# A blockwise scan with ten columns a state instead of eleven

## What is computed

```python
def step(h, inp):
    dA_t, dB_t, x_t, C_t, t = inp
    h = h * dA_t + dB_t * x_t[:, :, None]
    nrm = jnp.sqrt(jnp.sum(h * h, axis=(1, 2), keepdims=True))
    fac = jnp.minimum(20.0 / (nrm + 1e-08), 1.0)
    h = jnp.where(t % 10 == 0, h * fac, h)
    y = jnp.einsum('bdn,bn->bd', h, C_t) + D_param * x_t
    return (h, y)
```

## Time and profile before

| | |
|---|---|
| median of 3 runs | 1531.29 us (1530.69 to 1533.32) |
| the profiled execution, its own time | 1536.68 us |
| its span in the profile | 1534.8 us |
| mean granted TensorE clock | 0.991 |
| PE, DVE, ACT, POOL busy, share of the span | 95%, 82%, 73%, 61% |

### The profile page before, as it was taken

How to read it: one execution, slowest core, us unless ns; L and a number is a source line. 1 busy time by engine, 2 the same in 40 slices (tenths; PEclk the granted TensorE clock), 3 DMA queues, 4 the chain that set the end, 5 groups by cost and what they waited for, 6 DMA issues and landing times.

```text
span 1534.8 us, 25461 instructions
## 1 busy us (share of the span) xinstructions
PE 1455.1 (95%) x6902; PEld 1020.6 (66%) x6902; DVE 1255.2 (82%) x2526; ACT 1121.2 (73%) x2618; POOL 939.6 (61%) x956
## 2 busy tenths in 40 slices
PE   6999999999979999999999999999999998999998
PEld 5555555555467777777777777777666666677776
DVE  6685566745479999999999999999999998788884
ACT  4444455455999999999999999999999964334243
POOL 0224313432269999999999999999999997400000
PEclk9999999999999999999999999999999999999999
DMA  8215437453757667666666666666545447466420
GB/s 269 83 49 176 131 103 198 139 178 115 233 137 208 169 165 188 168 172 167 172 165 181 177 162 181 157 173 172 133 111 112 95 105 224 116 221 193 150 84 28
DMA packets 231557, 236.28 MB, mean 154 GB/s; under 512 B 46040, under 2 KB 197272, under 8 KB 231416
## 3 DMA queue, kind: packets, MB, share of 16 engines
q1 hardware_dynamic: 230472, 233.34, 54.4%
q10 hardware_dynamic: 944, 1.31, 0.2%
HBM read 136.31 MB, written 98.56 MB: 153 GB/s over the span
## 4 chain that ended last, share of the span: by engine, by line
DVE 35%; POOL 14%; PE 12%; issue 5%; DVEq 1%; POOLq 1%; DMA 1%; ACT 0%; SPq 0%; ACTq 0%
DVE h L1346 22%; POOL rc L1110 13%; DVE banks L1336 8%; PE banks L1495 4%; PE banks L1516 3%; PE banks L1526 3%; DVE qs L1330 2%; PE banks L1170 1%; DVEq L1344 1%; DMA ub<-scratch_ub 1%; DVE q_ln_st L1772 1%; DVE q_g L1681 1%; POOLq L1118 1%; DVE q_x L1653 1%; PE banks L1536 0%
## 5 line engine op out<-in xcount | busy, mean ns | idle before, releaser
L1346 DVE TENSOR_TENSOR_SCAN h<-decay,banks 128x352 f32<-128x352 f32 x820 | 710.4, 882 | 57.4 <-DVE banks L1336 2.9
L1121 POOL TENSOR_TENSOR hc<-h,bc 128x640 f32<-128x640 f32 x410 | 593.3, 1447 | 0.0
L1170 PE MATMUL banks<-hc,w_ident 128*128 128x320 f32 (+1 forms) x1664 | 526.6, 440 | 0.1
L1239 ACT ACTIVATE tb<-dtc,a 128x320 f32<-128x320 f32 (+1 forms) x832 | 417.2, 555 | 4.8 <-DVE x L612 4.8
L1170 PEld LDWEIGHTS banks<-hc,w_ident 128*128 128x128 f32 x1664 | 285.0, 191 | 70.7 <-issue 0.8
L1261 ACT ACTIVATE decay<-tb 128x640 f32<-128x640 f32 x410 | 294.9, 723 | 0.0
L1110 POOL TENSOR_TENSOR rc<-qs,w_mhalf 128x1 f32<-128x1 f32 x410 | 225.8, 551 | 110.5 <-DVE qs L1330 110.5
L1156 PE MATMUL banks<-ub 128*128 128x176 f32 x1640 | 273.5, 289 | 2.4 <-DMA ub<-scratch_ub 2.4
L1149 PEld LDWEIGHTS banks<-sc_ss,sc_ones 128*128 128x128 f32 x820 | 123.5, 189 | 158.2 <-ACT sc_sq L1250 152.2
L1156 PEld LDWEIGHTS banks<-ub 128*128 128x128 f32 x1640 | 217.6, 193 | 2.6 <-DMA ub<-scratch_ub 2.6
L1149 PE MATMUL banks<-sc_ss,sc_ones 128*128 128x1 f32 x820 | 151.8, 254 | 37.7 <-ACT sc_sq L1250 19.5
(11 more groups left out here) (133 smaller groups left out, 1818.5 us busy)
## 6 DMA issues: line engine op xcount, KB each, us to landing
ub<-scratch_ub SPq DMA_DIRECT2D x410, 107.5 KB
bc<-scratch_blk SPq DMA_DIRECT2D x205, 160.0 KB, 3.5
scratch_ub<-turned SPq DMA_DIRECT2D x64, 512.0 KB, 3.6
scratch_ub<-spread SPq DMA_DIRECT2D x64, 176.0 KB, 2.6
scratch_xc<-xc SPq DMA_DIRECT2D x8, 1024.0 KB, 4.8
scratch_sg<-sg SPq DMA_DIRECT2D x8, 1024.0 KB, 6.0
piece<-scratch_u SPq DMA_DIRECT2D x32, 256.0 KB, 4.0
q_ys<-scratch_y SPq DMA_DIRECT2D x8, 1024.0 KB, 5.7
```

The source lines that it names most:

```text
L1121: pool.tensor_tensor(hc[:, pl % 2, :, at * S:(at + 1) * S] .rearrange("p (c b n) e -> p c b n e", c=KE, b=B)[:, :, b], state(m)[:, :, 0:S] ...
L1170: mm = pe.matmul(banks[:, y_bank(p), 0:KE * B * wide], w.ident[:], rhs, start=(n == 0), stop=(n == N - 1))
L1239: act.activation(tanh_rows(c, r), dtc[:, c % 2, k * B:(k + 1) * B, 0:blocks_of(c) * S].rearrange("p b (k e) -> p k b e", e=S), ACT.Tanh, s ...
L1346: dve.tensor_tensor_scan(state(m).rearrange("p r e -> p (r e)")[:, half], decay[:, m % DRING, half], psI[m % B][:, half], 0.0, ALU.mult, A ...
```

## The change

The scan block shrinks to the ten times 10j+1 to 10j+10, so a row has W = 10 columns. What column 0 did is now done in three places. VectorE multiplies the last column of the unit before by the decay of the first time of the block (`first_step`, into `hd`). `carry` multiplies that by the factor and adds it to column 0 of the input in PSUM. And since the state at 10j+10 leaves the scan unscaled, its output has to be scaled later: all factors are kept (`rcs`), and GpSimd multiplies each tenth output by its factor in the post stage (`scale_ends`). The output at time 0 is made once (`first_output`). ScalarE makes the first decays of 4 blocks and both batches in one exp of 512 elements (`first_d`). The halves of the scan are 24 and 40 rows instead of 32 and 32. The decay ring has 5 places instead of 6.

```diff
-W = S + 1
+W = S
-DRING = 6
+DRING = 5
+FG = 4
+LEAD = 24
-    HR = NCH // 2
+    HALVES = (slice(0, LEAD), slice(LEAD, NCH))
...
 def scalar(act, pre, post):  # decays(m)
+            if k % FG == 0 and b == 0:
+                if group_of(j) >= 2:
+                    act.wait_ge(hd_ready, (j - (FG if k else (blocks_of(c - 1) - 1) % FG + 1)) * B)
+                dst, src = first_of_group(j)
+                act.activation(dst, src, ACT.Exp, scale=DTA_HALF / SHARP).then_inc(first_ready, 1)
             act.activation(
                 decay[:, m % DRING].rearrange("p (g i e) -> p g i e", g=DB, e=W)[:, :, :, 1:],
-                tanh_block(j, b), ACT.Exp, scale=DTA_HALF / SHARP).then_inc(decay_ready, 1)
+                tanh_block(j, b)[:, :, :, 1:], ACT.Exp, scale=DTA_HALF / SHARP).then_inc(decay_ready, 1)
...
         def carry(m):
-            b = m % B
+            j, b = m // B, m % B
+            dve.wait_ge(hd_ready, m + 1)
             dve.wait_ge(norm_ready, m + 1)
             dve.wait_ge(inp_ready, m + 1)
-            dve.tensor_scalar(inp(m)[:, :, 0], state(m - B)[:, :, S], rc[:, b:b + 1], None, ALU.mult
-                              ).then_inc(carry_ready, 1)
+            dve.scalar_tensor_tensor(out=inp(m)[:, :, 0], in0=hd[:, b, :], scalar=rcs[:, j, b:b + 1],
+                                     in1=inp(m)[:, :, 0], op0=ALU.mult, op1=ALU.add).then_inc(carry_ready, 1)
+
+        def first_step(m):
+            for x in range(2):
+                dve.wait_ge(h_ready[x], m + 1)
+            dve.wait_ge(first_ready, group_of(m // B) + 1)
+            dve.tensor_tensor(hd[:, m % B, :].rearrange("p (g i) -> p g i", i=GR),
+                              state(m - B)[:, :, W - 1].rearrange("p (g i) -> p g i", i=GR),
+                              first_decays(m // B, m % B), ALU.mult).then_inc(hd_ready, 1)
...
+        first_step(0)
         for m in range(UNITS):
             carry(m)
+            if m + 1 < UNITS:
+                first_step(m + 1)
             scan(m, 0)
             if B <= m + 1 < UNITS:
                 clamp(m + 1)
...
 def gpsimd(pool, post):  # scan stage
         def norm(m):
-            b = m % B
-            if m >= B:
-                pool.wait_ge(carry_ready, m - B + 1)
+            j, b = m // B, m % B
             pool.wait_ge(q_held, m + 1)
-            pool.tensor_tensor(rc[:, b:b + 1], qs[:, b:b + 1], w.mhalf[:, 0:1], ALU.pow).then_inc(norm_ready, 1)
+            pool.tensor_tensor(rcs[:, j, b:b + 1], qs[:, b:b + 1], w.mhalf[:, 0:1], ALU.pow).then_inc(norm_ready, 1)
...
+            if m == UNITS - 17:
+                post.scale_ends(pool, 0)
...
 def gpsimd(pool):  # post stage
+        scale_ends(pool, 1)
+        rstd(0)
         for i in range(TILES):
-            rstd(i)
+            if i + 2 < TILES:
+                scale_ends(pool, i + 2)
+            if i + 1 < TILES:
+                rstd(i + 1)
+
+    def scale_ends(pool, i):
+
+        j0 = -(-i * TT // S)
+        j1 = -(-(i + 1) * TT // S)
+        at = ys[i % 2][:].rearrange("p k (b t) -> p k b t", b=B)[:, :, :, j0 * S - i * TT::S]
+        pool.wait_ge(y_in[i % 2], 16 * (i // 2 + 1))
+        pool.tensor_tensor(at, at, scan.rcs[:, j0:j1].rearrange("p j b -> p b j").unsqueeze(1)
+                           .broadcast_to([P, KE, B, j1 - j0]), ALU.mult).then_inc(scan.ends_scaled, 1)
```

More of the change, by code:

```diff
@@ L700, in vector @@
                 scan.decay_scale(dve)
+                scan.first_output(dve)
                 post.residual_steps(dve)
@@ L728 @@
 Scan = namedtuple("Scan", """sync gpsimd tensor scalar vector load_first load_units tanhs decay_rates decay_scale masks
-    decay_ready y_out y_copied squares load_piece turn_piece high_piece low_piece store_piece ut_lo
+    first_output rcs ends_scaled decay_ready y_out y_copied squares load_piece turn_piece high_piece low_piece store_piece ut_lo
     spread_b store_b copy_bt b_split""")
@@ L808, in scan_stage @@
     qs = own.put("qs", [P, B])
-    rc = own.put("rc", [P, B])
+    rcs = own.put("rcs", [P, NB, B])
+    hd = own.put("hd", [P, B, NCH])
+    c0 = own.put("c0", [P, B, N, 2])
+    s0 = own.put("s0", [P, B])
+    y0 = own.put("y0", [P, KE * B])
     u0 = own.put("u0", [P, KE * B, 2])
@@ L814, in scan_stage @@
     h = second.put("h", [P, 2, B, NCH, W])
+    first_d = second.put("first_d", [P, 2, DB * FG * B * GR])
     hc = second.put("hc", [P, 2, ROWS, QB * S])
@@ L903, in load_first @@
         for b in range(B):
-            sp.dma_start(b0[:, b], dram["bc"][0:N, b:b + 1, 0:2].rearrange("n b t -> b n t")
-                         .broadcast_to([P, N, 2])).then_inc(s_in, 16)
+            for tile, n0 in ((b0, 0), (c0, N)):
+                sp.dma_start(tile[:, b], dram["bc"][n0:n0 + N, b:b + 1, 0:2].rearrange("n b t -> b n t")
+                             .broadcast_to([P, N, 2])).then_inc(s_in, 16)
         sp.wait_ge(blk_out, 32)
@@ L1344, in scan @@
                 dve.wait_ge(carry_ready, m + 1)
-            half = slice(x * HR * W, (x + 1) * HR * W)
+            half = slice(HALVES[x].start * W, HALVES[x].stop * W)
             dve.tensor_tensor_scan(state(m).rearrange("p r e -> p (r e)")[:, half], decay[:, m % DRING, half],
@@ L1636, in skip_first @@
         if k == 0:
-            dve.wait_ge(y_in[0], 16)
+            dve.wait_ge(scan.ends_scaled, 1)
         dve.wait_ge(scaled, k + 1)
@@ L1820, in _ @@
                 pre.gpsimd(pool, scan)
-                scan.gpsimd(pool)
+                scan.gpsimd(pool, post)
                 post.gpsimd(pool)
```

71 lines of the change are left out of this document (52 added, 19 removed).

## The result

The changed kernel takes **1801.54 us** (median of 4 runs, 1800.58 to 1802.44); the kernel before takes 1530.99 beside it. The ratio is 1.1772, with a 95% interval of 1.1756 to 1.1788. Its profiled execution took 1801.09 us around a span of 1799.2, so 264.4 us more than the span of before; the forecast had +267 for it.

The account below looks back on a forecast made before the run. Bound: the scan stage's loop through VectorE and GpSimd, 2.178 us a unit. New unit 1.77 + 0.20 + 0.58 + 0.28 = 2.83 us; 408 × 0.65 = +266 us, giving 1798 us; range 1735 to 1880.

Parts of the forecast that it names:

- Weigh, 0.51 and 1.447: GpSimd in the scan loop: weigh starts 0.51 us behind the power and lasts 1.447, to 1.96, still 640 elements.
- Carry: VectorE in the scan loop: after a second half of 0.91 us, carry starts at 0.68, so first_step is up at 0.94.
- The hold, released 0.19 before weigh's end: VectorE's first_step waits for weigh, begins in effect at 1.77 us, so VectorE stands still for about 0.8 us.
- The low end of the range: Product at 0.225 us and weigh's early release partly in proportion to its length, 0.33 instead of 0.19: unit 2.68, time 1735.
- Product, 0.20 of interval: VectorE's first_step: own time 0.28 us, next instruction starting about 0.08 before its end, so 0.20 of the unit.
- First half and clamp to power, 0.58 + 0.28: End of the scan unit: first half of 240 elements takes 0.58 us, then clamp, then 0.28 to the next power.
- The first rival (no meeting): Scan loop: first_step and weigh do not meet; VectorE's loop 2.02 us, unit 2.1, time 1515 us; chance 0.08.
- the chance of 0.06 for faster: Whole kernel: the forecast's chance that the change makes it faster, beside same 0.02 and slower 0.92.
- The clock rival: TensorE in the scan stage falls to half clock as it rests more; 1935 us with half the stage so; chance 0.08.
- The second rival's partial hold: Scan loop: weigh holds the ports for a part only; unit 2.2 to 2.6 us, some 1550 to 1700 us; chance 0.09.

Follow-up runs that it names:

- e10_flat: Kernel before with weigh reading the first 640 elements of the state in one piece instead of ten of each eleven columns; 1536.98 us.
- e2_add_sbuf: Kernel before with a product added behind the carry, the state's last column times an SBUF factor, result unused; 1879.81 us.
- e7_late24: Changed kernel with first_step moved from in front of the scan's first half to behind the clamp; 1604.22 us, ratio 1.0456.
- e6_wait_back: Changed kernel with the wait on the carry of two units before put back ahead of GpSimd's power; 1829.04 us.
- e1_psum: Changed kernel with first_step's second factor read from PSUM instead of first_d in SBUF, leaving out the first decay; 1540.16 us, 1.005 times before.

## Why the prediction was right

The range, the side and the mechanism held, and the number to 4 us. That it came so close is partly luck, since two terms were off by 0.08 to 0.10 us a unit and cancel; either alone would have moved the time by 30 to 40 us. By the steps, counted from the power:

1. *Weigh, 0.51 and 1.447.* The start is right (0.516). The length is 1.542: "it is still 640 elements" left out that the rows now touch, and e10_flat shows the price of that, 0.10. This is the step that failed: **+0.095**.
2. *Carry.* The second half's interval was given as 0.91 and is 0.89, and the carry starts at 0.74 instead of 0.68, since the clamp is nearer to the power. It takes 0.257, which is what the working took (0.26). None of it is on the path: the product is up 0.40 into weigh instead of 0.43, and its end does not move with that.
3. *The hold, released 0.19 before weigh's end.* Right, and firmer than it was put. Over 407 products the end lies 0.08 behind weigh's (0.078 to 0.087); with 0.27 of its own it begins in effect 0.19 before weigh's end. That beginning is worked out; the trace shows the ends. It is 0.08 for weighs of 1.20 us, of 1.44 (e2_add_sbuf) and of 1.54, and for products that were up 0.31, 0.39 or 0.56 into them. The low end of the range assumed a release in proportion to weigh's length; the distance is the same for all three lengths.
4. *Product, 0.20 of interval.* 0.19 by the timeline (1003.26 less 1003.07). Its own time is 0.27 where nothing holds it (e7_late24), near the 0.28 of the strided row and above the 0.224 of the formula, which the Trainium skill, "VectorE: DVE Perf Modes", section on the TRN2 errata, states for an fp32 add.
5. *First half and clamp to power, 0.58 + 0.28.* The half is 0.57. Clamp to power is 0.20: the diff takes a wait out ahead of the power, which the working did not price. e6_wait_back puts it back and finds 0.065 to 0.07. The rest goes with a clamp of 0.126 us instead of 0.134: e2_add_sbuf has the wait and a clamp of 0.127, and clamp to power is 0.27 there. **-0.08**.

The sum is 0.516 + 1.542 - 0.19 + 0.19 + 0.57 + 0.20 = 2.83. Weighing the rule of the Trainium skill against the row was worth its place: by a hold for the whole instruction, as that page has it, the forecast would have been 1876 us.

The first rival (no meeting) can now be checked, since e1_psum is that case. It gave 1515 us; its VectorE loop of 2.02 us is what the shorter units of that trace take, but it counted the exp of 512 at 0.62, by the line through plain exps, and the exp, which reads one column in ten, takes 1.11. What is off is the price of an element: the one exp of 128 there takes 0.43, so the elements between the two cost 1.8 ns each instead of 0.81. (No run has the same exp over neighbouring elements, so that the stride is the cause is likely, not shown.) The case's own time is 1540, just slower than before. So, as far as e1_psum stands for it, the change doesn't pay as written even with no hold at all: the chance of 0.06 for faster was too kind. The clock rival is refuted for this load: with TensorE 77% busy the granted clock stayed at 1.00. The second rival's partial hold does not occur: all 407 products that meet a weigh end 0.08 behind it. `scale_ends` and the first output cost nothing visible: from the end of the last scan to the end of the span it is 212.0 us, against 212.4 before, and the first carry comes 1.9 us earlier than before.

## What to carry to other kernels

Before an elementwise step is put on VectorE, look where its operands lie and what GpSimd runs then: here a product of 64 elements with two operands in SBUF, up behind the start of a long two-operand GpSimd instruction, ended just behind that instruction, and with one in PSUM it was not held. A product that replaces a column saves elements but adds an instruction whose inputs must be made, so price the strided exp and the changed row layout from rows of that shape, not from plain ones. Ask of each wait in the loop whether the order of another engine's list already implies it: one such wait was worth 1% here.

## What the runs showed of the hardware beyond that

- A second semaphore wait ahead of GpSimd's power cost 0.065 us, though satisfied for 3 to 5 us, in two pairs of kernels (clamp to power 0.206 to 0.271 with it added, 0.279 to 0.214 with it removed). With both waits the late one stood in an instruction of its own.
- GpSimd's product over 640 elements takes 1.447 us when it skips every eleventh column and 1.54 to 1.55 when its rows touch (e10_flat).
- ScalarE's exp over 512 elements takes 1.11 us at a stride of ten elements; the line through its exps of 64 and 640 gives 0.62.
- The held product ends 0.08 us behind GpSimd's weigh, for weighs of 1.20, 1.44 and 1.54 us; with 0.27 us of its own it is as if it began 0.19 before weigh's end.
- The wait of the held product counts as busy time in the profile: VectorE reads 100% busy from 1000 to 1100 us, and the product's records are 43.5 of these 100 us.
